# Loading x in one piece, issuing the bias late, and 44 unread matmuls ahead of the first products of a graph layer

## The reference

```python
def _L0_gnn_ref(input, adj, weight, bias):
    support = input @ weight
    mask = (adj != 0).astype(support.dtype)
    rank = jnp.cumsum(mask, axis=1)
    deg = rank[:, -1:]
    k = jnp.minimum(deg, 100.0)
    pos = rank - (deg - k)
    w = mask * jnp.where(pos > 0, 0.5 ** (k - pos), 0.0)
    return w @ support + bias
h = jnp.maximum(_layernorm(x, axis=-1), 0.0)
out = x + _L0_gnn_ref(h, adj, L0_gnn_weight, L0_gnn_bias)
```

## Time and profile before

| What | Value |
|---|---|
| Median of 3 runs (lowest, highest) | 219.22 us (218.03, 219.27) |
| Profiled execution: its own time, its span | 219.09 us, 216.5 us |
| Mean granted TensorE clock in it | 0.982 of full |
| PE busy, share of span | 197.1 us, 91% |
| DVE busy | 197.2 us, 91% |
| ACT busy | 160.9 us, 74% |
| POOL busy | 33.1 us, 15% |
| DMA queue of adj, share of 16 engines | 74.3% |

### The profile page before, as it was taken

The page is one execution under the profiler, slowest core; times in us unless marked ns, Lnnn a source line. Parts: engine busy times, 40 slices in busy tenths (PEclk is TensorE's granted clock), DMA queues, the critical chain, the costliest instruction groups (busy, mean ns, idle before and its releaser), DMA issues.

```text
span 216.5 us, 6393 instructions
## 1 busy us (share of the span) xinstructions
PE 197.1 (91%) x2740; PEld 188.1 (87%) x2740; DVE 197.2 (91%) x239; ACT 160.9 (74%) x303; POOL 33.1 (15%) x52
## 2 busy tenths in 40 slices
PE   0387598999899999999999999999999999999993
PEld 0287367898798999999999999999999999999993
DVE  0989989599989999999999999969999999999893
ACT  2441777697587778888787878788988899998720
POOL 8700011040010105050103060500000000000000
PEclk9999759999999999999999999999999999999999
DMA  5999999999999999999999999999996000000001
GB/s 181 189 215 212 215 215 216 218 216 217 215 212 216 215 215 215 212 221 218 215 215 220 216 215 217 215 219 215 219 215 147 15 3 3 12 15 3 12 3 42
DMA packets 8586, 36.11 MB, mean 167 GB/s; under 512 B 1648, under 2 KB 4464, under 8 KB 4464
## 3 DMA queue, kind: packets, MB, share of 16 engines
q0 software_dynamic: 4608, 33.56, 74.3%
q1 hardware_dynamic: 3280, 1.61, 3.1%
q10 hardware_dynamic: 672, 0.56, 0.8%
HBM read 68.22 MB, written 1.05 MB: 320 GB/s over the span
## 4 chain that ended last, share of the span: by engine, by line
PE 83%; DMA 5%; DVE 5%; ACT 3%; issue 2%; POOL 0%; DVEq 0%; POOLq 0%
PE acc L616 40%; PE chain L609 26%; PE chain L607 15%; DMA adj_b<-in_adj 5%; ACT powers L308 3%; DVE masks L363 2%; PE chain L595 2%; PE acc L575 1%; DVE acc L477 1%; DVE later L404 1%; DVE part L369 1%; DVE sums L369 0%; ACT support L282 0%; DVE sum_b L436 0%; DVE sum_a L431 0%
## 5 line engine op out<-in xcount | busy, mean ns | idle before, releaser
L308 ACT ACTIVATE powers<-chain 128x512 int16<-128x512 f32 (+1 forms) x279 | 148.2, 572 | 36.4 <-PE chain L609 33.7
L616 PE MATMUL acc<-support,powers 128*128 128x192 bf16 x1024 | 160.2, 246 | 2.7 <-ACT powers L308 2.4
L609 PE MATMUL chain<-diag_own,masks 128*128 128x128 bf16 x608 | 108.0, 221 | 0.0
L607 PE MATMUL chain<-diag_past,masks 128*128 128x128 bf16 x568 | 103.1, 221 | 1.6 <-ACT powers L308 1.6
L616 PEld LDWEIGHTS acc<-support,powers 128*128 128x128 bf16 x1024 | 95.9, 98 | 6.8 <-issue 5.0
L363 DVE TENSOR_SCALAR masks<-adj_b 128x4096 uint8<-128x4096 bf16 x32 | 72.7, 2281 | 3.3 <-DMA adj_b<-in_adj 3.0
L609 PEld LDWEIGHTS chain<-diag_own,masks 128*128 128x128 fp8e3 x608 | 60.0, 100 | 0.7 <-issue 0.6
L609 PE MATMUL chain<-diag_step,masks 128*128 128x128 bf16 x416 | 60.2, 219 | 0.0
L607 PEld LDWEIGHTS chain<-diag_past,masks 128*128 128x128 fp8e3 x568 | 56.1, 99 | 3.4 <-ACT powers L308 2.8
L230 POOL DMA_DIRECT2D adj_b<-in_adj x32 | 28.6, 898 | 105.9 <-DVE masks L363 105.2
L609 PEld LDWEIGHTS chain<-diag_step,masks 128*128 128x128 fp8e3 x416 | 39.6, 99 | 0.3
(11 more groups left out here) (47 smaller groups left out, 61.2 us busy)
## 6 DMA issues: line engine op xcount, KB each, us to landing
adj_b<-in_adj POOLq DMA_DIRECT2D x32, 1024.0 KB, 35.0
out<-x_sb SPq DMA_DIRECT2D x14, 64.0 KB, 4.5
x_sb<-in_x SPq DMA_DIRECT2D x1, 512.0 KB, 4.2
x_sb<-in_x ACTq DMA_DIRECT2D x1, 512.0 KB, 5.5
out<-x_sb SPq DMA_DIRECT2D x4, 32.0 KB, 9.2
bias_b<-in_L_gnn_bias ACTq DMA_DIRECT2D x1, 32.0 KB, 9.6
w<-in_L_gnn_weight SPq DMA_DIRECT2D x2, 16.0 KB, 8.5
```

What stands on the lines that cost most here:

```text
L308: nc.scalar.activation(powers[:, c, b, cols].bitcast(i16), chain[c][:, cols], ACT.Relu, bias=(MAX_NEIGH + 1) * STEP).then_inc(powers_ready ...
L607: nc.tensor.matmul(chain[c][:, at:at + P], column(n, t + 1), diag_past[:, :], start=False, stop=False, skip_group_check=True)
L609: return nc.tensor.matmul(chain[c][:, at:at + P], column(n, t), diag_own[:, :] if marked else diag_step[:, :], start=False, stop=True, ski ...
L616: return nc.tensor.matmul(acc[u % ACCS][:, k * 3 * D:(k + 1) * 3 * D], powers[:, u % FLIGHT, s + 1 if k < MARKS[u] else s, at:at + P], sup ...
```

## The change

x comes in one load of whole 8 KB rows from SP, on one semaphore. The two loads of the weight move from SP to ScalarE. The load of the bias moves from ScalarE's start to SP, where it waits until mask(0) is done. A helper `spin(n)` issues n matmuls of the constant tile `minus` with itself into the PSUM bank `spare`, which no instruction reads after the transposes; it stands with 8 at the end of slot 1, 18 and 8 ahead of the two take-offs of slot 2, and 10 at the end of slot 3. The other lines turn the constant `BATCH` into a table with 4 for each unit, take out a branch for an empty table `SIGNED`, and add tables `OWN_BEATS` (empty) and `LEADS` (zeros) that the loops consult; `differ` waits for the powers as well as for the floor.

```diff
         def _(sp):
-            sp.dma_start(half_of(x_sb, 0), half_of(x.rearrange("(p t) d -> p t d", t=T), 0)).then_inc(x_loaded[0], 16)
-            sp.wait_ge(w2_zeroed, 2)
-            sp.dma_start(w2[0:D, 0:D], weight).then_inc(weight_loaded, 16)
-            sp.dma_start(w2[D:2 * D, D:2 * D], weight).then_inc(weight_loaded, 16)
+            sp.dma_start(x_sb[:, :, :], x.rearrange("(p t) d -> p t d", t=T)).then_inc(x_loaded, 16)
+
+            sp.wait_ge(mask_ready, 1)
+            sp.dma_start(bias_b[:, :], bias.rearrange("(a d) -> a d", a=1).to_broadcast([P, D]))\
+              .then_inc(bias_loaded, 16)
...
         def _(act):
-            act.dma_start(half_of(x_sb, 1), half_of(x.rearrange("(p t) d -> p t d", t=T), 1)).then_inc(x_loaded[1], 16)
-            act.dma_start(bias_b[:, :], bias.rearrange("(a d) -> a d", a=1).to_broadcast([P, D]))\
-               .then_inc(bias_loaded, 16)
-            act.wait_ge(w2_zeroed, 1)
+            act.wait_ge(w2_zeroed, 2)
+            act.dma_start(w2[0:D, 0:D], weight).then_inc(weight_loaded, 16)
+            act.dma_start(w2[D:2 * D, D:2 * D], weight).then_inc(weight_loaded, 16)
             nc.scalar.activation(warm[:, :], warm[:, :], ACT.Sqrt)
...
             def differ(u, j):
                 c = u % FLIGHT
-                dve.wait_ge(floored[c], batches_until(u) + j + 1)
+                dve.wait_ge(powers_ready[c], taken_until(u) + BATCH[u] * (j + 1) + 1)
+                done = floors_until(u) + sum(i <= j for i in to_floor(u))
+                if done:
+                    dve.wait_ge(floored[c], done)
...
             def row_sums(f):
-                dve.wait_ge(x_loaded[f], 16)
+                dve.wait_ge(x_loaded, 16)
...
+            def spin(n):
+
+                for _ in range(n):
+                    nc.tensor.matmul(spare[:, 0:P], minus[:, :], minus[:, :], start=True, stop=True)
...
                 if g == 0:
                     make_support(3)
+                if g == 1:
+                    spin(8)
                 if g == 2:
+                    spin(18)
                     take_off(0, 0)
+                    spin(8)
                     take_off(1, 0)
+                if g == 3:
+                    spin(10)
```

More of the change, by code:

```diff
@@ L33, in gnn_decay_kernel @@
     FLIGHT = 3
-    BATCH = 4
     LOADS = 8
@@ L55, in gnn_decay_kernel @@
     LAGS = [7, 4, 10, 9, 9, 9, 10, 8, 9, 9, 8, 12, 11, 11, 11, 10, 9, 8]
-    SIGNED = {}
-    PIECES = 8
+    BATCH = [4, 4, 4, 4, 4, 4, 4, 4, 4, 4, 4, 4, 4, 4, 4, 4, 4, 4]
+    OWN_BEATS = {}
+    LEADS = [0, 0, 0, 0, 0, 0, 0, 0, 0, 0, 0, 0, 0, 0, 0, 0, 0, 0]
     NU = len(SIZES)
@@ L69, in taken_until, with by_vector, first_of, to_floor @@
         return sum(TAKEN[v] for v in range(u % FLIGHT, u, FLIGHT))
+    def by_vector(u, b):
+        return u in OWN_BEATS and OWN_BEATS[u][0] <= b < OWN_BEATS[u][1]
+    def first_of(u, j):
+        return BATCH[u] * j + (1 if j else 0)
+    def to_floor(u):
+        if MARKS[u] == SIZES[u]:
+            return []
+        return [j for j in range(STEPS[u] // BATCH[u])
+                if not all(by_vector(u, b) for b in range(first_of(u, j), BATCH[u] * (j + 1) + 1))]
+    def floors_until(u):
+        return sum(len(to_floor(v)) for v in range(u % FLIGHT, u, FLIGHT))
     def batches_until(u):
-        return sum(STEPS[v] // BATCH for v in range(u % FLIGHT, u, FLIGHT) if MARKS[v] < SIZES[v])
+        return sum(STEPS[v] // BATCH[v] for v in range(u % FLIGHT, u, FLIGHT) if MARKS[v] < SIZES[v])
     def halved_until(u):
@@ L130, in gnn_decay_kernel @@
         split = acc
-        x_loaded = [sem(f"x_loaded{f}") for f in range(2)]
+        x_loaded = sem("x_loaded")
         bias_loaded = sem("bias_loaded")
@@ L156, in gnn_decay_kernel @@
         xb_ready = sem("xb_ready")
-        signs_ready = sem("signs_ready")
         mask_ready = sem("mask_ready")
@@ L284, in part @@
                                      ACT.Copy).then_inc(part_ready[i], 1)
[L286 to L293, removed]
             def weigh(u, b):
@@ L322, in _ @@
                     for u in range(c, NU, FLIGHT):
-                        if 0 <= g - STARTS[u] <= STEPS[u]:
+                        if 0 <= g - STARTS[u] <= STEPS[u] and not by_vector(u, g - STARTS[u]):
                             weigh(u, g - STARTS[u])
-                for n in SIGNED:
-                    if 0 <= g - SIGNED[n] < PIECES:
-                        signs(n, g - SIGNED[n])
                 if g == 1:
@@ L351, in mask @@
             def mask(n):
[L353 to L358, removed]
                 dve.wait_ge(adj_loaded[n % LOADS], 16 * (n // LOADS + 1))
@@ L406, in scan, with weigh @@
                                              ALU.add, ALU.add).then_inc(later_ready, 1)
+            def weigh(u, b):
+                c = u % FLIGHT
+                dve.wait_ge(chain_ready[c], taken_until(u) + b + 1)
+                nc.vector.tensor_scalar(powers[:, c, b, plain(u)].bitcast(i16), chain[c][:, plain(u)],
+                                        (MAX_NEIGH + 1) * STEP, STEP, ALU.add, ALU.max).then_inc(powers_ready[c], 1)
             def floor(u, j):
                 c = u % FLIGHT
-                first, last = BATCH * j + (1 if j else 0), BATCH * j + BATCH
+                last = BATCH[u] * (j + 1)
                 dve.wait_ge(powers_ready[c], taken_until(u) + last + 1)
-                bits = powers[:, c, first:last + 1, plain(u)].bitcast(i16)
+                bits = powers[:, c, first_of(u, j):last + 1, plain(u)].bitcast(i16)
                 nc.vector.tensor_scalar(bits, bits, STEP, None, ALU.max).then_inc(floored[c], 1)
@@ L416, in differ @@
                 c = u % FLIGHT
-                dve.wait_ge(floored[c], batches_until(u) + j + 1)
-                before = powers[:, c, BATCH * j:BATCH * j + BATCH, plain(u)]
-                after = powers[:, c, BATCH * j + 1:BATCH * j + BATCH + 1, plain(u)]
+                dve.wait_ge(powers_ready[c], taken_until(u) + BATCH[u] * (j + 1) + 1)
+                done = floors_until(u) + sum(i <= j for i in to_floor(u))
+                if done:
+                    dve.wait_ge(floored[c], done)
+                before = powers[:, c, BATCH[u] * j:BATCH[u] * (j + 1), plain(u)]
+                after = powers[:, c, BATCH[u] * j + 1:BATCH[u] * (j + 1) + 1, plain(u)]
                 nc.vector.tensor_tensor(before, before, after, ALU.subtract).then_inc(weights_ready[c], 1)
@@ L516, in _ @@
             for g in range(SLOTS + 4):
+                for u in OWN_BEATS:
+                    if by_vector(u, g - STARTS[u]):
+                        weigh(u, g - STARTS[u])
                 for u in range(NU):
-                    if MARKS[u] < SIZES[u] and g - STARTS[u] in range(BATCH + 1, STEPS[u] + 2, BATCH):
-                        floor(u, (g - STARTS[u] - 1) // BATCH - 1)
+                    if (g - STARTS[u] - 1) % BATCH[u] == 0 and (g - STARTS[u] - 1) // BATCH[u] - 1 in to_floor(u):
+                        floor(u, (g - STARTS[u] - 1) // BATCH[u] - 1)
                 if g == 15:
@@ L524, in _ @@
                 for u in range(NU):
-                    to = STARTS[u] - g
+                    to = STARTS[u] - LEADS[u] - g
                     if u >= 3 and to == 8 and FIRST[u] > 3:
@@ L547, in _ @@
                 for u in range(NU):
-                    if MARKS[u] < SIZES[u] and g - STARTS[u] in range(BATCH + 1, STEPS[u] + 2, BATCH):
-                        differ(u, (g - STARTS[u] - 1) // BATCH - 1)
+                    if MARKS[u] < SIZES[u] and g - STARTS[u] in range(BATCH[u] + 1, STEPS[u] + 2, BATCH[u]):
+                        differ(u, (g - STARTS[u] - 1) // BATCH[u] - 1)
         @block.tensor
         def _(pe):
+            def spin(n):
+                for _ in range(n):
+                    nc.tensor.matmul(spare[:, 0:P], minus[:, :], minus[:, :], start=True, stop=True)
             def turn_h(i):
@@ L632, in before_products @@
                     pe.wait_ge(powers_ready[c], taken_until(u) + s + 1)
-                elif s % BATCH == 0:
-                    pe.wait_ge(weights_ready[c], batches_until(u) + s // BATCH + 1)
+                elif s % BATCH[u] == 0:
+                    pe.wait_ge(weights_ready[c], batches_until(u) + s // BATCH[u] + 1)
             def counted(u, s):
```

## The result

| | before | changed |
|---|---|---|
| Median of ten runs (lowest, highest) | 218.41 us (217.53, 219.27) | 216.88 us (216.41, 217.53) |
| Ratio, with 95% interval | | 0.9913 (0.9895, 0.9931) |
| Profiled execution, its span | 219.09 us, 216.5 us | 217.53 us, 215.0 us |
| Granted clock, mean over the span | 0.982 | 0.997 |

The change gains 0.9% by the ratio of the table; the medians differ by 1.5 us (0.7%), the two profiled executions by 1.6 us. The kernel before is 0.8 us faster in ten runs than in the three shown first. By the prediction's bound of 1% this is no change, by its interval it is a gain. The changed kernel's profiled execution is the slowest of its ten.

What follows compares the result with a forecast made beforehand. Ahead of a nearly fixed TensorE matmul block, the chain of waits from the first adj load and the low clock bound the time. Prologue 0.6 plus clock 1.75 take 2.35 us off the span: 216.9 us, range 216.0 to 219.2.

Steps and rivals of the forecast that it cites:

- the prediction's bound of 1%: Whole kernel: a difference under 1% (2.2 us, so 217.0 to 221.4) is about what a measurement can tell from none.
- The 44 cost nothing: TensorE's pauses: 44 added matmuls, 2.5 us of TensorE, end before the waits they stand in front of, costing nothing.
- The clock stays up: TensorE's low stretch, 24.64 to 31.46 us: filling pauses keeps full clock, gain 1.75 us; bounds 0 and 1.75.
- The walk at full clock: Low stretch retraced with ScalarE's durations kept: first product at 30.45 instead of 32.21, 1.75 us gained.
- Rival C: Low stretch: the clock falls all the same, earlier or later, leaving 218.6 us; chance 0.20.
- The prologue, 0.6: Start, x and bias loads: mask(0) starts 0.6 us earlier; bounds a gain of 0.9 and a loss of 1.5.
- rival B: Prologue gives nothing, x landing 1 us later or first tile no earlier: 217.5 us; chance 0.15.
- D: Start: x's large packets take turns with adj's, x landing over 2.7 us later: 221.4 or 223.1 us; chance 0.06.
- The adj tiles gain 0.7: adj loads: with bias and weight out of the way, the first tile lands 0.7 us earlier (nothing to 0.9).
- Can the block take it?: Matmul block: whether it can start 2.35 us earlier; base(3) has 2.08 us plus the tiles' 0.7, enough.
- The cap's own sum: base(9): slack 1.72 us; with adj earlier by less than 0.6, gain capped at 1.7 plus adj's gain.
- The sum: Whole kernel: gains of 0.6 and 1.75, together 2.35 us, give 216.9; as rival A, 216.2 to 217.7, chance 0.50.

Runs made afterwards that it cites:

- the second set: The changed kernel run once more, unaltered, beside three other kernels on the same chip: 216.80 us, 0.9907 of the kernel before.

## Why the prediction was right, and where its sum was not

- **The 44 cost nothing.** Right: spacing and places as forecast, and no instruction behind them late.
- **The clock stays up.** Right, in each of the ten executions (0.997 to 1.0), and the matmuls alone do it, for 1.75 us by the medians. The walk at full clock gave 1.75 us; in the trace the stretch from mask(0) to the first product shrank by 2.46 - 0.66 = 1.80. Rival C is dead. Whether all of the gain comes through the granted clock is open: in three executions of the kernel before it stayed up by itself, and they took 218.4 us on average, against 217.1 with the matmuls alone. No profile was taken of such an execution.
- **The prologue, 0.6.** Right in size, 0.66: row_sums(0) started at 5.58 (forecast 5.4), mask(0) at 12.46 (12.5). The late x of rivals B and D did not come. Which move made it is not settled: the late bias alone gives mask(0) at 12.19, whole rows with the bias in front give 12.48, and both kernels have the weight's move as well.
- **The adj tiles gain 0.7.** Wrong. Tile 0 landed 1.4 us earlier, but from tile 3 on they came 0.2 to 0.5 us later in the first profile (in the second, tiles 4 and 8 within 0.2 of before). I moved the bias's load to where nothing waits for it, and costed it at nothing. The queue it moved into feeds a resource that is busy all the time, and 0.9 us of it went to 32 KB. By the first engine that is done, the lead shrank from 1.25 us at tile 0 to 0.27 at tile 3, so even without what follows 0.7 was not to be had. The second part of the lateness, a slowest engine that trails by another half microsecond, was there with the matmuls alone too and is not explained.
- **Can the block take it?** This step failed with the one above: base(3)'s slack was 2.08 plus the tiles' 0.7, and the 0.7 were -0.2, so the lead of 2.46 was cut to 1.83 there. At base(9) slack was down to 0.06 us. The cap's own sum, 1.72 less the 0.43 by which mask(10) was late, would have left 1.3; the lead there was 1.76, because VectorE's scans of unit 9 ended 0.1 earlier than before all the same. The idea that it follows the loads one for one was wrong by 0.5 us. No single base is shown to be the cap: base(3), base(5) and base(9) each held TensorE.
- **The sum.** 2.35 us forecast; measured 1.5 by the medians, and 2.05 in the second set. What is short is the prologue's 0.6, which hardly counts on top of the matmuls' 1.75. The time is the one that rival B worked out from, the matmuls' gain alone, though not for B's reason: x and mask(0) came about as forecast. That the time came out at 216.9 all the same is luck: the three runs of before (219.22) were 0.8 us slow against ten (218.41), which made up for the 0.8 us that the gain fell short. In 53 further executions of the kernel before, 26 have the long low stretch (mean clock near 0.983) and a mean of 219.1 us, 24 the half one (0.992) and 218.3, 3 none and 218.4. The trace I predicted from showed the long one, and half the executions had less to gain: the matmuls alone, at 217.1, are 2.0 us below the first group and 1.2 below the second. That the median gain was 1.75 rests on the share of each. I had named the spread of the three runs under rival C and not drawn that from it.

## What to carry to other kernels

When one transfer stream keeps all DMA engines busy, moving a small load out of the prologue moves its cost to that stream, it does not remove it (0.9 us of adj in either place here): count its pieces, and cut these, before choosing its place. A lead won at the start is worth no more than the smallest slack behind it, and that slack is counted against when the tiles land. What the profile of one execution shows of the clock may be one of several ways in which the executions go; look at the granted clock of more than one before pricing it.

## What the runs showed of the hardware that was not expected

The granted clock of 1.00 in the first 17 us is not what TensorE ran at. TensorE's timeline of the kernel before:

```profile
15.27 3.16 PE L568 MATMUL acc<-w,powers 128*128 128x128 f32 x16
...
19.20 1.11 PE L568 MATMUL acc<-w,powers 128*128 128x128 f32 x8
```

Sixteen take 3.16 us, eight of the same take 1.11. Single records show 0.213 us from start to start up to 17.8 us and 0.11 behind that, the two levels of the clock. The trace's first clock record is a rise at 17.81 us; the page fills the time before it with full speed. In the changed kernel the rise is at 15.87. No wait for these products shows in the timelines, so it cost nothing that can be seen here. But in these two traces TensorE's prologue ran at 1.2 GHz, whatever that row says.

A load of 32 KB in 128 pieces of 256 B took 0.9 us from a saturated stream, as much as 0.2 MB of it, and one packet of 256 B took nothing that can be seen (tile 4's first engine at 30.14, against 30.08 with no load of the bias).
